# Expert stage of an attention and mixture-of-experts layer on one core: a fourth scatter-add in flight, and expert weights loaded in four pieces

## The reference

```
xn  = layernorm(x)
out = x + attention(xn) + ffn(xn)
attention: 16 heads of width 32, one shared key and value head, rotary positions, causal softmax, projection
ffn:  scores = sigmoid(xn gate^T); per token the 8 best of 32 experts, out of the 2 best of 4 groups
      weight   = scores of the 8, divided by their sum, times 2.5
      x_lat    = xn fc1^T                                   (512 -> 256)
      y_lat[t] = sum over chosen e of weight[t,e] * relu(x_lat[t] w1[e]^T)^2 w2[e]^T      (256 -> 256 -> 256)
      routed   = y_lat fc2^T;   shared = relu(xn up^T)^2 down^T
```

## Time and profile before

| | us |
|---|---|
| median of 3 runs (range) | 1802.2 (1796.65 to 1810.25) |
| the profiled execution, its own time | 1801.09 |
| its span in the trace | 1799.3 |
| PE busy, share of the span | 1642.5, 91% |
| DVE busy | 1196.9, 67% |
| ACT busy | 1068.8, 59% |
| POOL busy | 825.5, 46% |

### The profile page before, as it was taken

One profiled execution on the slowest core, in us unless ns is written; L12 is line 12 of the kernel. 1 busy time (PEld: TensorE's weight loads), 2 busy tenths in 40 slices (PEclk: granted clock), 3 DMA queues, 4 the chain that ended last, 5 costly groups with the idle time before them and its releaser, 6 DMA issues.

```text
span 1799.3 us, 40017 instructions
## 1 busy us (share of the span) xinstructions
PE 1642.5 (91%) x10806; PEld 1389.0 (77%) x10806; DVE 1196.9 (67%) x3661; ACT 1068.8 (59%) x2791; POOL 825.5 (46%) x670
## 2 busy tenths in 40 slices
PE   5833999999999999999999998999999999999989
PEld 5822777777777777787777776888888988889977
DVE  6868877767868778677677784454445544455557
ACT  2322775766757757677577574666556665566642
POOL 0042532433424424334244241577677766777850
PEclk9966999999999999999999999999999999999999
DMA  7983533434334334334343334688888887888894
GB/s 279 369 308 79 153 99 117 143 103 130 124 98 144 116 110 137 106 123 132 97 149 119 122 99 138 145 162 178 171 182 171 168 181 167 175 169 153 138 258 164
DMA packets 189150, 277.86 MB, mean 154 GB/s; under 512 B 34232, under 2 KB 130623, under 8 KB 186372
## 3 DMA queue, kind: packets, MB, share of 16 engines
q0 software_dynamic: 60352, 92.59, 23.9%
q1 hardware_dynamic: 73636, 117.19, 22.0%
q10 hardware_dynamic: 54944, 65.52, 12.4%
HBM read 123.93 MB, written 131.76 MB: 142 GB/s over the span
## 4 chain that ended last, share of the span: by engine, by line
PE 57%; DMA 14%; DVE 12%; issue 7%; ACT 2%; POOL 1%; DVEq 1%; POOLq 0%; ACTq 0%; SPq 0%
DMA sums<-e_y,e_where 13%; PE m_psT L1190 7%; PE e_psH L1566 6%; PE e_psY L1577 6%; PE m_psU L64 5%; PE m_psU L66 4%; PE m_psU L65 4%; PE m_psS L1173 4%; PE m_psO L1210 4%; PE m_psY L64 4%; PE m_psY L66 4%; PE m_psY L65 4%; DVE m_sc L999 3%; PE e_psX L1551 2%; POOL sums L1531 1%
## 5 line engine op out<-in xcount | busy, mean ns | idle before, releaser
L1531 POOL DMA_INDIRECT sums<-e_y,e_where x287 | 445.7, 1553 | 202.7 <-DVE e_y L1490 123.7
L777 POOL DMA_INDIRECT slot_rows<-m_row,slots x256 | 268.4, 1048 | 553.0 <-ACT m_sc L854 509.0
L854 ACT ACTIVATE m_sc<-m_sc,m_low 128x512 f32<-128x512 f32 (+3 forms) x512 | 283.8, 557 | 154.8 <-DVE m_low L999 153.5
L1577 PE MATMUL e_psY<-e_w,e_ht 128*128 x1148 | 302.8, 387 | 25.9 <-ACT e_ht L1438 25.9
L1566 PE MATMUL e_psH<-e_xt,e_w_of 128*128 128x128 f32 x2296 | 310.3, 279 | 3.3 <-ACT e_xt L1427 3.3
L999 DVE CUSTOM_DVE_ANT_0 m_sc<-m_psS,cst 128x512 f32<-128x512 f32 (+3 forms) x512 | 229.6, 485 | 90.8 <-PE m_psS L1173 89.6
L1566 PEld LDWEIGHTS e_psH<-e_xt,e_w_of 128*128 128x128 f32 x2296 | 283.4, 194 | 5.6 <-ACT e_xt L1427 4.0
L1433 ACT ACTIVATE e_w_of<-e_w 128x512 f32 x287 | 180.8, 630 | 130.9 <-issue 122.4
L1577 PEld LDWEIGHTS e_psY<-e_w,e_ht 128*128 128x128 f32 x1148 | 198.8, 193 | 45.8 <-issue 29.6
L1487 DVE TENSOR_SCALAR e_where<-e_row,e_shifts 128x1 uint32<-128x1 uint32 x287 | 61.4, 214 | 214.0 <-DMA sums<-e_y,e_where 180.4
L1190 PE MATMUL m_psT<-cst,m_sc 128*128 128x128 f32 x1280 | 199.8, 277 | 2.0 <-ACT m_pt L865 2.0
(11 more groups left out here) (201 smaller groups left out, 3162.8 us busy)
## 6 DMA issues: line engine op xcount, KB each, us to landing
e_row<-slot_rows ACTq DMA_DIRECT2D x287, 144.5 KB, 3.5
m_qs<-m_qhi SPq DMA_DIRECT2D x256, 64.0 KB, 2.0
e_w<-in_w SPq DMA_DIRECT2D x64, 256.0 KB, 4.6
f_xt<-in_x SPq DMA_DIRECT2D x8, 1024.0 KB, 9.3
xnt_hi<-f_hi SPq DMA_DIRECT2D x8, 1024.0 KB, 4.4
xnt_lo<-f_lo SPq DMA_DIRECT2D x8, 1024.0 KB, 7.7
m_qs<-m_qlo SPq DMA_DIRECT2D x128, 64.0 KB, 2.0
sums<-empty POOLq DMA_DIRECT2D x32, 256.0 KB
```

The costliest lines, as they stand in the source:

```text
L777: pool.indirect_dma_start(out=xs, out_offset=bass.IndirectOffsetOnAxis(ap=slots_sb[:, g, k:k + 1], axis=0), in_=row[g % 2][:, :], in_offse ...
L854: nc.scalar.activation(cols, cols, ACT.Exp, bias=low[:, h % 2, i:i + 1], scale=-1.0, accum_out=total[:, h % 2, i:i + 1]).then_inc(exp_done, 1)
L1531: pool.indirect_dma_start(out=both_sums, out_offset=bass.IndirectOffsetOnAxis(ap=where[u % NY][:, 0:1], axis=0), in_=y[u % NY][:, :], in_o ...
L1577: mm = pe.matmul(psY[u % 2][:, 0:LAT], ht[u % 2][:, c * P:(c + 1) * P], w_f[:, bass.ds(e * (2 * W) + (W + c * LAT), LAT)], start=(c == 0), ...
```

## The change

- `FLIGHT` goes from 3 to 4: four semaphores `added`, and with `NY = 2 * FLIGHT` eight buffers `e_y` and `e_where` instead of six. POOL waits for tile u-4, DVE for the buffers of tile u-8, and for tile u-6 (or u-2) and tile u-7 (or u-3) by the table: with four adds in flight, that of tile u-3 can overlap with tile u's.
- The packed number holds two flags instead of a count, and `weigh` works out two counts in registers and waits twice. `Routing.tables` computes the flags for u-2 and u-3.
- An expert's weights are loaded in four pieces of 32 partitions, two DMAs of 64 KB for each piece, and piece q waits for tile `end + q`, so one piece follows each finished tile. The loads of `partial` come behind the fourth piece.
- `NP` goes from 6 to 5: one `e_early` buffer fewer, one `partial` load more in the loop.

```
-FLIGHT = 3
+FLIGHT = 4
...
-        link(nc.vector.tensor_tensor(due_f, expert_f[:, 0:3], expert_f[:, 3:6], ALU.subtract))
-        link(nc.vector.tensor_scalar(due_f, due_f, 2.0, 16.0 * E, ALU.is_ge, ALU.mult))
-        link(nc.vector.tensor_tensor(due_f, due_f, cst[:, COL["due"]], ALU.add))
-        link(nc.vector.tensor_tensor(self.due_i, due_f, expert_f[:, 0:3], ALU.add))
+        for n in range(2):
+            link(nc.vector.tensor_tensor(due_f[:, 3 * n:3 * n + 3], expert_f[:, 0:3], expert_f[:, 3 * n + 3:3 * n + 6], ALU.subtract))
+            link(nc.vector.tensor_scalar(due_f[:, 3 * n:3 * n + 3], due_f[:, 3 * n:3 * n + 3], 2.0, float(E << n), ALU.is_ge, ALU.mult))
+        link(nc.vector.tensor_tensor(due_f[:, 0:3], due_f[:, 0:3], due_f[:, 3:6], ALU.add))
+        link(nc.vector.tensor_tensor(self.due_i, due_f[:, 0:3], expert_f[:, 0:3], ALU.add))
...
-NP, RC = 6, 5
+NP, RC = 5, 5
+WP = 4
...
+            def load_part(k, q):
+                cols, rows_of = slice(k * W, (k + 1) * W), slice(q * P // WP, (q + 1) * P // WP)
+                for n, w in enumerate((w1, w2)):
+                    sp.dma_start(w_sb[rows_of, k, n, :], w[rows_of, cols]).then_inc(w_in[k % 2], 16)
...
-                sp.wait_ge(y_done, end_of(k - AHEAD) + BASE)
-                load(k)
+                end = end_of(k - AHEAD)
+                for q in range(WP):
+                    sp.wait_ge(y_done, end + (BASE + q))
+                    load_part(k, q)
...
-                due, e = packed // E, packed % E
+                e = packed % E
                 if not first(i, u, NY):
                     landed(dve, i, u - NY)
-                if not first(i, u, 2 + FLIGHT):
-                    dve.wait_ge(added[(u - 2) % FLIGHT], due)
-                elif u >= 2:
-                    landed(dve, i, u - 2)
+                for n, two_on in ((2, packed // E % 2), (3, packed // (2 * E))):
+                    if not first(i, u, n + FLIGHT):
+                        dve.wait_ge(added[(u - n) % FLIGHT], two_on * 16 + 16 * ((u - n) // FLIGHT))
+                    elif u >= n:
+                        landed(dve, i, u - n)
```

More of the change, by code:

```diff
@@ L40 @@
 BASE = 16
-WIDTHS = dict(ident=P, tri=P, mask=S, cosq=S, sinq=S, cosk=S, sink=S, token=G, earlier=NG * NG, tile=6, due=3, lane=1, spare=1)
+WIDTHS = dict(ident=P, tri=P, mask=S, cosq=S, sinq=S, cosk=S, sink=S, token=G, earlier=NG * NG, tile=9, lane=1, spare=1)
 COL, _at = {}, 0
@@ L324, in __init__ @@
         self.beats = res[:, 1056:1568].rearrange("p (g a b) -> p g a b", a=NG, b=NG)
-        self.owner = res[:, 1056:1248].rearrange("p (t e) -> p t e", e=E)
+        self.owner = res[:, 1056:1344].rearrange("p (t e) -> p t e", e=E)
         self.offset = by_expert(res[:, 1248:1504])
@@ L330, in __init__ @@
         self.pad = [res[:, 1856:1888], res[:, 1888:1920]]
-        self.expert_f, self.due_f, self.shift_f = res[:, 1920:1926], res[:, 1926:1929], res[:, 1929:1932]
+        self.expert_f, self.due_f, self.shift_f = res[:, 1344:1353], res[:, 1353:1359], res[:, 1929:1932]
         self.token_sum = res[:, 1936:1968]
@@ L560, in tables @@
         expert_f, due_f = self.expert_f, self.due_f
-        link(nc.vector.tensor_tensor(self.owner, self.end.unsqueeze(1).broadcast_to([P, 6, E]),
-                                     cst[:, COL["tile"]].unsqueeze(2).broadcast_to([P, 6, E]), ALU.is_le))
+        link(nc.vector.tensor_tensor(self.owner, self.end.unsqueeze(1).broadcast_to([P, 9, E]),
+                                     cst[:, COL["tile"]].unsqueeze(2).broadcast_to([P, 9, E]), ALU.is_le))
         link(nc.vector.tensor_reduce(expert_f, self.owner, AX.X, ALU.add))
@@ L1357, in sp_program @@
             after(sp, "q_done")
+            def load_part(k, q):
+                cols, rows_of = slice(k * W, (k + 1) * W), slice(q * P // WP, (q + 1) * P // WP)
+                for n, w in enumerate((w1, w2)):
+                    sp.dma_start(w_sb[rows_of, k, n, :], w[rows_of, cols]).then_inc(w_in[k % 2], 16)
             def load(k):
-                cols = slice(k * W, (k + 1) * W)
-                for n, w in enumerate((w1, w2)):
-                    sp.dma_start(w_sb[:, k, n, :], w[:, cols]).then_inc(w_in[k % 2], 16)
+                for q in range(WP):
+                    load_part(k, q)
             def arrived(k):
-                sp.wait_ge(w_in[k % 2], 32 * (k // 2 + 1))
+                sp.wait_ge(w_in[k % 2], 32 * WP * (k // 2 + 1))
                 sp.sem_inc(w_ready, 1)
@@ L1477, in weigh @@
             def weigh(i, u):
-                packed = dve.value_load(table[0:1, bass.ds(i * PER + (DUE_AT + u), 1)], min_val=0, max_val=16 * E * SLOT_TILES)
-                due, e = packed // E, packed % E
+                packed = dve.value_load(table[0:1, bass.ds(i * PER + (DUE_AT + u), 1)], min_val=0, max_val=4 * E - 1)
+                e = packed % E
                 if not first(i, u, NY):
                     landed(dve, i, u - NY)
-                if not first(i, u, 2 + FLIGHT):
-                    dve.wait_ge(added[(u - 2) % FLIGHT], due)
-                elif u >= 2:
-                    landed(dve, i, u - 2)
+                for n, two_on in ((2, packed // E % 2), (3, packed // (2 * E))):
[3 more added lines that the diff above has]
+                        landed(dve, i, u - n)
                 dve.wait_ge(row_in[u % NR], i * (16 * PER // NR) + 16 * (u // NR + 1))
@@ L1639, in constant_table @@
     tile = np.arange(3)[None] + 3 * p[:, None]
-    c[:, COL["tile"]] = np.concatenate([tile, tile - 2], 1)
-    c[:, COL["due"]] = 16 * E * np.maximum((tile - 2) // FLIGHT, 0)
+    c[:, COL["tile"]] = np.concatenate([tile, tile - 2, tile - 3], 1)
     c[:, COL["lane"]] = p[:, None]
```

## The result

The kernel after takes 1756.95 us in the median of four runs (1755.36 to 1757.76), against 1801.21 us for the kernel before in the same measurement: a ratio of 0.9746 with an interval of 0.9713 to 0.9779. I had forecast 1762, with a range up to 1787.

The account below looks back on a forecast made before the run. PE idles behind late adds, held by POOL's limit of three in flight beside weight loads. From 1801.1 us: -38.9 in the loop, -2.3 and -2.0 at the end, +0.6, +0.4, +3 give 1762 us; range 1753 to 1775, wider to 1787.

Parts of the forecast that it names:

- The excess of 42.7 us: Tile loop: all 287 tiles start within 608.4 us, where 286 steps at 1.978 us are 565.7; 42.7 can be won.
- POOL's limit of adds in flight: POOL's adds: three in flight; landings up to 8.57 us beside weight loads delay the next issue, and PE stops.
- The limits 5.0 and 7.0 us: POOL's adds: the time from issue to landing before POOL falls behind the floor, with three and four in flight.
- Lumps add L - 4.65 and L - 6.51: POOL's lag per weight load, L being the landing time, with three and four in flight; full tiles win back 0.12 us each.
- With either alone I would expect most of the gain.: Tile loop: the fourth add and the four weight pieces cover each other, so each by itself brings most of the gain.
- Three us for stalls behind the largest lumps: Tile loop: +3 us for stalls that remain behind the largest loads after the change.
- The end: After the last `result`: 2.3 us less waiting for an add, 2.0 (0 to 3) less clock loss on PE.
- SP's queue before the stage: Before the expert stage: 40 issues replace 10, about 17 us, taken as 0; 3 us if not covered.
- DVE's registers: `weigh` on DVE's sequencer: 0.4 us more per tile (0.19 to 0.72), hidden within 0.83 us; 0.4 once at the end.
- The tables, +0.6 us: DVE near 183 us: two more linked steps at 0.2 and two wider ones at 0.1, with nothing to hide them.
- Half the stalls stay: Rival, tile loop: the faster loop keeps adds slow for longer, half of 38.9 us stays: 1781 us; chance 0.10.
- Pieces slow every add: Rival, DMA queues beside POOL's adds: small loads keep adds slow on nearly every tile, 78 us: 1837 us; chance 0.05.

Follow-up runs that it names:

- one more load: The changed kernel with the packed table value loaded twice in each `weigh`, against the kernel before: 1789.67 us, ratio 0.9897, loop 592.3 us.
- the two cuts: The kernel before with weights in four pieces over four tiles, 32 partitions by 2 KB or 128 by 1 KB: ratios 0.9873 and 0.9878.

## Why the prediction was right, and where it was not

The forecast was 39.2 us below the profiled execution of before (1801.1), and it came 45.7 below. By its steps:

- **The excess of 42.7 us as what can be won in the loop.** Right. Of it 40.9 were won, and what remains is start-up. The starts of `result` span 567.5 us, just below the 568 to 575 that I had named as the sign.
- **Who causes it: POOL's limit of adds in flight, with landings late beside weight loads.** Right. The limit is shown by two runs that differ from after in one thing each: POOL back at three loses most of the gain (0.9939), DVE back at u-5 loses none in the loop (0.9726). The place of the late landings is shown by the trace of before, 75 of 79 beside weight loads. DVE's row of 158.8 us in the earlier trace rows, which the prediction took for waiting for adds, is to a large part the sequencer's own work. "Put down to DVE" was the correct warning about POOL's row.
- **The limits 5.0 and 7.0 us.** They hold up in the table: 87 landings over 5.0 in after cost nothing with four in flight, while 79 over 5.0 with three go with the 38.9 us outside the start-up.
- **Lumps add L - 4.65 and L - 6.51, and the lag goes at 0.12 us a tile.** The prediction made of this an estimate of 46 us, against 38.9. It counted one late add for each of 27 lumps, and there were 79 over 5.0, so that it came so near is in part luck. The same arithmetic over all measured landings gives 604.8 us for the loop of before, against 608.4.
- **"With either alone I would expect most of the gain."** True for the fourth add, all of it; false for the pieces, about half. The step that failed is "the largest lump falls, and mostly below 6.5". It does: 24 landings over 7.0 become none. But with three in flight 6.5 is not the limit, 5.0 is, and as many landings as before lie above it. The half gain comes from being less far above it; the recurrence, fed with these landings, gives 581.0 for a loop of 589.8.
- **Three us for stalls behind the largest lumps.** None are left; the 277 steps after the start-up run at 1.974 us. This term, 1.1 us from a floor that is 0.004 us lower on 286 steps, and 0.9 us of start-up (2.9 where I left 3.8) are 5.0 us of the 6.5 by which the forecast was too high. The rest is the end and the tables, below.
- **The end.** I had -2.3 and -2.0 and + 0.4, in sum -3.9; measured -4.6. The first matmuls behind the tiles follow after 1.30 us of idling, where it was 3.27, and the four take 0.77 us instead of 1.11. The run with DVE at u-5 shows that most of this hangs on DVE's wait, not on POOL's: there the end takes 61.1 us.
- **SP's queue before the stage.** 19.9 us instead of 17, hidden as said: the table is asked for at 1104.37, and the first `result` starts no later.
- **DVE's registers.** I took 0.4 from a bracket of 0.19 to 0.72, and 0.25 were measured, hidden as said. The room of 0.83 us held: with one more load the addition is 0.25 + 0.62 = 0.87, and the loop just passes the floor. That load's expectation failed on its price, not on the room. It also shows that the change sits nearer to DVE's bound than "hidden" sounds. Some 0.6 us a tile are left, less than one more value load.
- **The tables, +0.6 us.** Not seen: the first `result` is 0.3 us earlier. It was too small to matter. Whether it was covered is not shown.
- **The rivals.** Half the stalls stay: no. Pieces slow every add: no, in after 4 landings of 224 are over the 7.0 from which this rival decides, and no difference between the two cuts was seen. The prediction said of `m_qs` that nothing ran beside it; POOL's scatters into `slot_rows` and other loads ran in the same stretch (300 to 1000 us, 121 GB/s in the mean), so its 2.0 us spoke more strongly against this rival than it claimed. DVE as the bound: no, but one value load away. Only moved: no, the wait is gone from PE.

## What to carry to other kernels

In this kernel, k adds in flight, issued 1.98 us apart, hid every landing up to k x 1.98 us less the 0.92 us from a landing to the next issue. Before working on shorter landings, count how many landings of the trace lie above that limit for k and for k + 1. Here one more in flight put all but a few under it, and the care taken with the size of the competing loads brought nothing more. The row of the engine that waits for the limit may name an earlier, innocent producer. And a row "engine waits for a DMA" can hold the engine's own register work: compare it with the sequencer's instructions, over the same number of tiles, before you read its total.

## What was not expected of the hardware

- A value load on DVE's sequencer from a table in SBUF cost 0.62 us a time: 0.30 for the load, 0.19 for the registers behind it, the rest in the assertion and gaps. Two more of them for each tile made this kernel 10% slower than before.
- Of the adds of 128 x 256 f32 in the kernel before, a twentieth land within 3.7 us, and the longest takes 8.57. The median moves little with the size of the loads (4.59 before, 4.69 with the pieces alone, 4.29 with four in flight and whole loads); the tail does.
- The length of one stall does not tell whether the granted clock falls. In before's loop it fell to the lower level five times (1.2 GHz), at stalls of 1.87, 2.27, 2.15, 2.06 and 1.86 us before a `result`. It did not fall at stalls of 2.10, 1.95, 1.94 and another one of 1.87. Two stalls of the same length, from PE's timeline of before:

```profile
1286.96 1.13 PE L1577 MATMUL e_psY<-e_w,e_ht 128*128 x4 [1.87 <-ACT e_ht L1438]
...
1334.17 1.95 PE L1577 MATMUL e_psY<-e_w,e_ht 128*128 x4 [1.87 <-ACT e_ht L1438]
```
